# Routing tables of a mixture-of-experts stage: row masks with the pairs innermost, in four pieces

## The chip, the cores and the metric

One core of a Trainium2 chip runs the whole program in one launch. The metric is the time of an execution on the device in microseconds (us); the runs shown are compared by their median. The engines are TensorE (matrix products), Vector, Scalar, GpSimd and Sync (which only issues transfers). In the profile's rows they are PE (PEld for its weight loads), DVE, ACT, POOL and SP.

## The reference

The input has 8 images of 256 channels and 16 x 16 points. A convolution block comes first; its result is added to x. Then every one of the 2048 points is a token of 256 numbers, and a mixture of 8 experts is applied:

```python
S = jax.nn.sigmoid(xt @ Wg)                       # 2048 tokens x 8 experts
G, I = jax.lax.top_k(S, 2)
h = jax.nn.gelu(jnp.einsum('nd,edf->enf', xt, W1) + b1[:, None, :])
y = jnp.einsum('enf,efd->end', h, W2) + b2[:, None, :]
combine = jnp.zeros((N, E)).at[jnp.arange(N)[:, None], I].add(G)
out = jnp.einsum('ne,end->nd', combine, y)
```

So only two experts count for a token. The kernel computes just these: 4096 pairs of a token and a choice.

## The kernel before, in words

**Stages.** The convolution block runs until about 85 us. Then the routing is worked out, and from about 116 us the experts run, tile by tile. Each tile has up to 128 pairs of one expert; there are 39 tiles, and the tables have 40 columns (TCOL). For each tile GpSimd gathers the token rows from memory (`xn_rows`) by row number, TensorE turns them (`turn`), Scalar and Vector round them into a high and a low 16-bit part (`turned_hi`, `rows_T`), TensorE does both layers (`first`, `second`), and GpSimd adds the rows to the output by the same row numbers.

**Routing.** A token sits on a partition (128) in one of 16 blocks (NBLK). With two choices there are 32 pairs per partition, numbered q = choice x 16 + block. Vector works out, for each pair, its tile number and its row in the tile (`place16[:, 1]` and `place16[:, 0]`). Then it builds masks with compares in 16-bit numbers:

- `pay[:, :, 0, :]`: for each pair, 40 numbers, 1 at its tile (L1326). `pay[:, :, 1, :]` is the same times the token's number (L1333), in two halves by choice.
- `hot`: for each pair, 128 numbers, 1 at its row (L1330), in two halves by choice.

TensorE's token table (L839) adds up, over the 32 pairs, hot of a pair (the stationary operand, 128 x 128) times its payload (40 columns). The result has the token's number at each row and tile. Vector turns it into row numbers (`idx`, L1340 and L1342), for which GpSimd's first gather waits (L522). Behind the table TensorE has 16 products of constants that keep it busy (L847), then the first `turn` (L853).

**Later.** The gates of the chosen experts go the same way: Vector multiplies the tile masks by the gates' high and low parts (`gate_pay`, L1369), and a second table with 80 columns (again L839) runs on TensorE ahead of the fourth step of the experts.

**What sets the order.** Each engine has its own list of instructions, in the order of the code, and waits on counters. On Vector, `link` makes an instruction's successor wait for it. Between the row numbers and the first gathered tile Vector splits expert weights into parts (`split_lo`, L972), and Scalar does so ahead of it (`split_hi`, L550). Sync's list (L424 to L446) writes the normalized rows (`rows_out`) and loads the weight quarters of 512 KB (`load`). GpSimd's list begins with memsets, copies the identity (L457) and pads the images (L473).

Of the kernel before, what the change touches and what calls it, by code (L numbers as in the profile page):

```python
# [27 lines left out]
ALU = mybir.AluOpType  # L28
# [3 lines left out]
F16 = mybir.dt.float16  # L32
# [4 lines left out]
P = 128  # L37
# [3 lines left out]
NBLK = NTOK // P  # L41
# [32 lines left out]
NSTG = 4  # L74
# [9 lines left out]
POOL_PADS = 6  # L84

# [21 lines left out]
def build(nc, x_tok, const, const16, params, w1, w2, b2, out):  # L107
    with ExitStack() as ctx:
# [3 lines left out]
        def sem(name):  # L112
            return ctx.enter_context(nc.semaphore(name))
# [47 lines left out]
        def place(n, at, size):  # L161

            return wt[:, n * EXPERT + at:n * EXPERT + at + size]
# [4 lines left out]
        hot = place(3, 0, 2 * NBLK * P).rearrange("p (q r) -> p q r", r=P)  # L168
# [4 lines left out]
        pay = late[:, 0:2560].bitcast(F16).rearrange("p (q v i) -> p q v i", v=4, i=TCOL)  # L173
# [132 lines left out]
        sel_done = sem("sel_done")  # L306
        prefix_mm = sem("prefix_mm")
        pay_done = sem("pay_done")
        hot_done = sem("hot_done")
        table_mm = sem("table_mm")  # L310
# [58 lines left out]
        def _(sp):  # L369
# [80 lines left out]
        def _(pool):  # L450
# [3 lines left out]
            nc.gpsimd.memset(minus_half[:, :], -0.5)  # L454
            g = nc.gpsimd
# [90 lines left out]
        def _(act):  # L546
# [136 lines left out]
        def _(pe):  # L683
# [150 lines left out]
            def table(v, n, bank):  # L834

                for k in range(2 * NBLK):
                    if k % NBLK == 0:
                        pe.wait_ge(hot_done, k // NBLK + 1 if v == 1 else 3)
                    m = pe.matmul(ps[:, bank, 0:n * TCOL], hot[:, k, :], pay[:, k, v:v + n, :].rearrange("p v i -> p (v i)"),  # L839
                                  start=(k == 0), stop=(k == 2 * NBLK - 1))  # L840
                m.then_inc(table_mm, 1)

            table(1, 1, 7)


# [106 lines left out]
            for n in range(TILES + 2):  # L952
                if n == 3:
                    table(2, 2, 7)
                step(n)
# [3 lines left out]
        def _(dve):  # L959
# [347 lines left out]
            def choose(dst, src):  # L1307
# [13 lines left out]
            dve.wait_ge(c16_in, 16)  # L1321
            iota16, tiles16 = c16[:, C16["iota"]], c16[:, C16["tiles"]]
            over_tiles = lambda x, n: x.unsqueeze(2).broadcast_to([P, n, TCOL])
            flat = lambda x: x.rearrange("p a k -> p (a k)")
            link(v.tensor_scalar(place16[:, 0], minus_row, -1.0, None, ALU.mult))
            v.tensor_tensor(out=pay[:, :, 0, :], in0=tiles16.unsqueeze(1).broadcast_to([P, 2 * NBLK, TCOL]),  # L1326
                            in1=over_tiles(flat(place16[:, 1]), 2 * NBLK), op=ALU.is_equal).then_inc(pay_done, 1)
            for a in range(TOP_K):
                half = slice(a * NBLK, (a + 1) * NBLK)
                v.tensor_tensor(out=hot[:, half, :], in0=iota16.unsqueeze(1).broadcast_to([P, NBLK, P]),  # L1330
                                in1=place16[:, 0, a].unsqueeze(2).broadcast_to([P, NBLK, P]), op=ALU.is_equal)
                dve.wait_ge(pay_done, 1)
                v.tensor_tensor(out=pay[:, half, 1, :], in0=pay[:, half, 0, :], in1=over_tiles(tok16[:, :], NBLK),  # L1333
                                op=ALU.mult).then_inc(hot_done, 1)
# [31 lines left out]
            def gate_pay():  # L1366

                for n in (2, 3):
                    ins = v.tensor_tensor(out=pay[:, :, n, :], in0=pay[:, :, 0, :],  # L1369
                                          in1=over_tiles(flat(place16[:, n]), 2 * NBLK), op=ALU.mult)  # L1370
                ins.then_inc(hot_done, 1)
# [133 lines left out]
```

## Time and profile before

| | us |
|---|---|
| median of 3 runs | 338.26 |
| lowest and highest | 337.83, 339.22 |
| the profiled execution | 339.53 |
| its span, first to last instruction | 337.6 |

| engine | busy, share of the span |
|---|---|
| TensorE | 302.4 us, 90% |
| Vector | 249.6 us, 74% |
| Scalar | 179.6 us, 53% |
| GpSimd | 157.1 us, 47% |

The chain that ended last is on TensorE for 73% of the span and on Vector for 13%. TensorE's share is an average: between about 95 and 108 us it does almost nothing, and it is then granted the lower clock of its two. Durations in the rows are those of the profiled execution.

### The profile page before, as it was taken

What the parts mean: (1) busy time and instruction counts of PE and PEld (TensorE: products, weight loads), DVE (VectorE), ACT (ScalarE), POOL (GpSimd) and SP (SyncE); (2) the same over time, 40 slices, a digit from 0 to 9 for tenths busy, and PEclk for the clock granted to TensorE, in tenths of its full rate; (3) what the DMA queues carried; (4) which work ended last, traced back from release to release, by engine and by line L of the source; (5) the groups of instructions that cost most, each with busy time, mean ns of one, the idle gap of its engine ahead of it and who ended that gap; (6) DMA issues with size and microseconds to landing.
All of it is one profiled execution on the core that took longest, in us unless ns stands there. A gap on an engine that the chain in (4) does not pass through costs nothing.

```text
span 337.6 us, 8684 instructions
## 1 busy us (share of the span) xinstructions
PE 302.4 (90%) x3050; PEld 228.4 (68%) x3050; DVE 249.6 (74%) x596; ACT 179.6 (53%) x507; POOL 157.1 (47%) x162
## 2 busy tenths in 40 slices
PE   7999999999412898999999999999999999999960
PEld 7787534567311496888888888888888888877730
DVE  4898796779899699878888888888756464665430
ACT  4557484625816175676666767676444535354310
POOL 2315912456410822664745474757545363544331
PEclk9999999999855799999999999999999999999995
DMA  7500000011578384878687778674353433334310
GB/s 220 173 2 1 2 0 1 0 63 67 190 235 241 80 277 150 206 201 213 188 206 194 214 183 232 160 199 73 76 84 65 81 66 69 70 53 60 55 17 2
DMA packets 36361, 39.41 MB, mean 117 GB/s; under 512 B 8448, under 2 KB 32992, under 8 KB 36320
## 3 DMA queue, kind: packets, MB, share of 16 engines
q1 hardware_dynamic: 29344, 29.56, 29.5%
q0 software_dynamic: 6976, 9.31, 16.1%
q8 instruction: 25, 0.41, 0.5%
q14 instruction: 16, 0.13, 0.1%
HBM read 29.74 MB, written 9.11 MB: 115 GB/s over the span
## 4 chain that ended last, share of the span: by engine, by line
PE 73%; DVE 13%; DMA 8%; issue 2%; ACT 0%; POOLq 0%; SPq 0%; POOL 0%
PE ps L914 16%; PE ps L899 8%; PE ps L903 8%; PE ps L901 8%; PE ps L915 8%; DMA out<-fb,idx 7%; PE ps L758 6%; PE ps L739 4%; PE ps L853 2%; PE ps L767 2%; PE ps L771 2%; PE ps L774 2%; PE ps L847 2%; DMA cst<-const 2%; PE ps L711 1%
## 5 line engine op out<-in xcount | busy, mean ns | idle before, releaser
L676 ACT ACTIVATE fb<-ps,b1t 128x128 f32<-128x128 f32 (+7 forms) x312 | 81.7, 373 | 82.7 <-issue 81.0
L914 PE MATMUL ps<-wt,fb 128*128 x312 | 117.0, 379 | 0.0
L899 PE MATMUL ps<-fb,wt 128*128 128x128 f16 (+7 forms) x624 | 114.3, 214 | 2.6 <-DVE fb L1364 2.6
L903 PE MATMUL ps<-fb,wt 128*128 128x128 f16 (+7 forms) x624 | 114.3, 214 | 0.0
L901 PE MATMUL ps<-fb,wt 128*128 128x128 f16 (+7 forms) x624 | 114.2, 214 | 0.0
L532 POOL DMA_INDIRECT out<-fb,idx x39 | 64.3, 1649 | 93.7 <-DVE s2c L1407 54.8
L915 PE MATMUL ps<-wt,fb 128*128 x312 | 85.0, 272 | 0.0
L899 PEld LDWEIGHTS ps<-fb,wt 128*128 x624 | 61.0, 98 | 32.9 <-issue 3.1
L901 PEld LDWEIGHTS ps<-fb,wt 128*128 x624 | 60.4, 98 | 3.3
L522 POOL DMA_INDIRECT fb<-xn_rows,idx x39 | 50.3, 1291 | 25.3 <-DVE idx L1342 12.8
L903 PEld LDWEIGHTS ps<-fb,wt 128*128 x624 | 60.4, 98 | 0.0
L1394 DVE SCALAR_TENSOR_TENSOR fb<-fb 128x1024 f16<-128x1024 f32 (+7 forms) x39 | 44.2, 1133 | 1.3
L1392 DVE TENSOR_SCALAR fb<-fb 128x1024 f16<-128x1024 f32 (+7 forms) x39 | 25.3, 647 | 26.1 <-ACT fb L676 25.4
L972 DVE SCALAR_TENSOR_TENSOR wt<-wt 128x1024 f16<-128x1024 f32 x32 | 38.1, 1216 | 0.0
L550 ACT ACTIVATE wt<-wt 128x1024 f16<-128x1024 f32 x32 | 34.1, 1100 | 5.9 <-DMA wt<-w 5.9
L1404 DVE SCALAR_TENSOR_TENSOR fb<-b2t,ps 128x256 f32<-128x256 f32 (+7 forms) x39 | 16.3, 419 | 25.9 <-PE ps L915 24.7
L914 PEld LDWEIGHTS ps<-wt,fb 128*128 128x128 f16 x312 | 30.5, 98 | 2.7
L915 PEld LDWEIGHTS ps<-wt,fb 128*128 128x128 f16 x312 | 30.5, 98 | 0.3
L758 PE MATMUL ps<-wt,fb 128*96 128x512 f32 x48 | 21.8, 599 | 0.0
L647 ACT ACTIVATE fb<-ps 128x256 f16<-128x256 f32 (+7 forms) x39 | 16.0, 411 | 10.4 <-PE ps L853 10.4
L500 POOL TENSOR_TENSOR fb<-cst,fm 128x256 f32<-128x256 f32 x16 | 10.7, 689 | 21.9 <-PE ps L774 12.9
L1407 DVE CUSTOM_DVE_ANT_0 fb<-ps,fb,gates 128x256 f32<-128x256 f32 (+7 forms) x39 | 18.8, 483 | 1.4
(208 smaller groups left out, 390.4 us busy)
## 6 DMA issues: line engine op xcount, KB each, us to landing
wt<-w SPq DMA_DIRECT2D x32, 512.0 KB, 4.2
b2t<-b SPq DMA_DIRECT2D x39, 128.0 KB, 3.4
out<-xt SPq DMA_DIRECT2D x8, 256.0 KB, 2.1
xn_rows<-wt SPq DMA_DIRECT2D x8, 256.0 KB, 3.3
xt<-x_tok SPq DMA_DIRECT2D x4, 256.0 KB, 4.7
xt<-x_tok SPq DMA_DIRECT2D x2, 512.0 KB, 7.6
b1t<-params SPq DMA_DIRECT2D x39, 4.0 KB, 2.4
fb<-xn_rows,idx POOLq DMA_INDIRECT x39, 3.7
```

Of the source, the lines that this page charges most:

```text
L522: nc.gpsimd.indirect_dma_start(out=xg[0:ROWS[i], g, :], out_offset=None, in_=xn_rows, in_offset=bass.IndirectOffsetOnAxis(ap=idx[0:ROWS[i] ...
L532: nc.gpsimd.indirect_dma_start(out=out, out_offset=bass.IndirectOffsetOnAxis(ap=idx[0:ROWS[i], i:i + 1].bitcast(U32), axis=0), in_=yb[0:RO ...
L550: nc.scalar.activation(quarter(h, 0), staged(h), ACT.Copy, scale=WS).then_inc(hi_done, 1)
L676: a = nc.scalar.activation(hid[:, s, f * P:f * P + ROWS[n]], h_ps(s)[:, f * P:f * P + ROWS[n]], ACT.Gelu_apprx_tanh, bias=b1t[:, n % NBIAS ...
L758: m = pe.matmul(ps[0:96, TAP_BANK[u], :], tapw[:, k, :], xln_pad[:, 2 * u:2 * u + 2, 1:1 + H, k:k + W], start=(k == 0), stop=(k == TAPS - 1))
L899: pe.matmul(dst, hi, xT[:, s, c * P:c * P + rows], start=(c == 0 and f % 4 == 0), stop=False, skip_group_check=True)
L901: pe.matmul(dst, hi, xT[:, s, (2 + c) * P:(2 + c) * P + rows], start=False, stop=False, skip_group_check=True)
L903: m = pe.matmul(dst, lo, xT[:, s, c * P:c * P + rows], start=False, stop=(c == DC - 1), skip_group_check=True)
L914: pe.matmul(y_ps(s), hhi[:, s, f * P:(f + 1) * P], w, start=(f == 0), stop=False)
L915: m = pe.matmul(y_ps(s)[:, 0:C], hlo[:, s, f * P:(f + 1) * P], hi, start=False, stop=(f == FC - 1))
L972: v.scalar_tensor_tensor(out=quarter(h, 1), in0=staged(h), scalar=WS, in1=quarter(h, 0), op0=ALU.mult, op1=ALU.subtract).then_inc(lo_done, 1)
L1394: v.scalar_tensor_tensor(out=lo, in0=full_h, scalar=HS, in1=hi, op0=ALU.mult, op1=ALU.subtract)\
```

## The change

`hot` and `pay` change their layout: the pair number q is innermost, so that column r of pair k lies 32 numbers (64 bytes) from column r + 1. The compare's other operand, which was a constant row read again for each pair, is now written out once at the program's start by two iotas on GpSimd (`iota_wide`, 128 x 8, and `tiles_wide`, 40 x 32). The row masks are made in four pieces of 8 pairs, each with a signal of its own, for which the token table waits; the tile mask and the token payload are made whole ahead of them. The gates' payload gets a tile of its own, `gpay`, in which the tile numbers stay innermost, and a signal of its own. Two moves go with it: Sync writes the last block of normalized rows behind two weight quarters and not four, and Scalar does the sigmoid of the logits and the following table load behind two weight quarters and not four.

```diff
+QUART = 2 * NBLK // 4
...
-        hot = place(3, 0, 2 * NBLK * P).rearrange("p (q r) -> p q r", r=P)
+        hot = place(3, 0, 2 * NBLK * P).rearrange("p (r q) -> p r q", q=2 * NBLK)
+        iota_wide = place(3, wide, P * QUART).rearrange("p (r k) -> p r k", k=QUART)
+        tiles_wide = place(3, wide + P * QUART, TCOL * 2 * NBLK).rearrange("p (i q) -> p i q", q=2 * NBLK)
...
-        pay = late[:, 0:2560].bitcast(F16).rearrange("p (q v i) -> p q v i", v=4, i=TCOL)
+        pay = late[:, 0:1280].bitcast(F16).rearrange("p (v i q) -> p v i q", v=2, i=TCOL)
+        gpay = late[:, 1280:2560].bitcast(F16).rearrange("p (q v i) -> p q v i", v=2, i=TCOL)
...
-            for h in range(NSTG):
+            for h in range(DC):
                 load(h)
             rows_out(B - 1)
+            for h in range(DC, NSTG):
+                load(h)
...
+            nc.gpsimd.iota(iota_wide, [[1, P], [0, QUART]], base=0, channel_multiplier=0,
+                           allow_small_or_imprecise_dtypes=True)
+            nc.gpsimd.iota(tiles_wide, [[1, TCOL], [0, 2 * NBLK]], base=0, channel_multiplier=0,
+                           allow_small_or_imprecise_dtypes=True).then_inc(wide_set, 1)
...
-            for h in range(QUARTERS_FIRST):
+            for h in range(DC):
                 split_hi(h)
             act.wait_ge(logit_done, 2)
             nc.scalar.activation(sgl[:, :, :], lg[:, :, :], ACT.Sigmoid, scale=1.0 / XS).then_inc(sigl_done, 1)
             nc.scalar.activation(scrap[:, :], eps_c, ACT.Gelu_apprx_tanh)
+            for h in range(DC, QUARTERS_FIRST):
+                split_hi(h)
...
+                    if k % QUART == 0:
+                        pe.wait_ge(hot_done, k // QUART + 1)
+                    m = pe.matmul(ps[:, 7, 0:TCOL], hot[:, :, k], pay[:, 1, :, k], start=(k == 0), stop=(k == 2 * NBLK - 1))
...
+                pe.wait_ge(gpay_done, 1)
+                for k in range(2 * NBLK):
+                    m = pe.matmul(ps[:, 7, 0:2 * TCOL], hot[:, :, k], gpay[:, k, :, :].rearrange("p v i -> p (v i)"),
...
-            for a in range(TOP_K):
-                half = slice(a * NBLK, (a + 1) * NBLK)
-                v.tensor_tensor(out=hot[:, half, :], in0=iota16.unsqueeze(1).broadcast_to([P, NBLK, P]),
-                                in1=place16[:, 0, a].unsqueeze(2).broadcast_to([P, NBLK, P]), op=ALU.is_equal)
...
+            over_tiles = lambda x: x.unsqueeze(1).broadcast_to([P, TCOL, 2 * NBLK])
+            dve.wait_ge(wide_set, 1)
+            v.tensor_tensor(out=pay[:, 0], in0=tiles_wide, in1=over_tiles(flat(place16[:, 1])),
+                            op=ALU.is_equal).then_inc(pay_done, 1)
+            dve.wait_ge(pay_done, 1)
+            v.tensor_tensor(out=pay[:, 1].rearrange("p i (a k) -> p i a k", a=TOP_K),
...
+            for j in range(4):
+                part_of = slice(j * QUART, (j + 1) * QUART)
+                v.tensor_tensor(out=hot[:, :, part_of], in0=iota_wide,
+                                in1=flat(place16[:, 0])[:, part_of].unsqueeze(1).broadcast_to([P, P, QUART]),
+                                op=ALU.is_equal).then_inc(hot_done, 1)
...
-                    ins = v.tensor_tensor(out=pay[:, :, n, :], in0=pay[:, :, 0, :],
-                                          in1=over_tiles(flat(place16[:, n]), 2 * NBLK), op=ALU.mult)
+                    ins = v.tensor_tensor(out=gpay[:, :, n - 2, :], in0=pay[:, 0].rearrange("p i q -> p q i"),
+                                          in1=flat(place16[:, n]).unsqueeze(2).broadcast_to([P, 2 * NBLK, TCOL]),
+                                          op=ALU.mult)
```

On Vector, the list between the places of the pairs and the row numbers was this (`place` holds tile and row numbers, `c` the 16-bit constants, `wt` the space where masks and payloads lie):

```order
L1325 TENSOR_SCALAR place<-gates 128x32 [waits c16_in,dve_step]
L1326 TENSOR_TENSOR wt<-c,place 128x32x40 [waits dve_step]
L1330 TENSOR_TENSOR wt<-c,place 128x2048
L1333 TENSOR_TENSOR wt<-wt,tok 128x16x40 [waits pay_done]
L1330 TENSOR_TENSOR wt<-c,place 128x2048
L1333 TENSOR_TENSOR wt<-wt,tok 128x16x40 [waits pay_done]
L1337 TENSOR_TENSOR lg<-lg,trs 128x128 [waits trs_done]
```

The same place on Vector now (line numbers are those of the changed kernel):

```order
L1345 TENSOR_SCALAR place<-gates 128x32 [waits dve_step]
L1347 TENSOR_TENSOR wt<-wt,place 128x1280 [waits wide_set,dve_step]
L1350 TENSOR_TENSOR wt<-wt,tok 128x1280 [waits pay_done]
L1355 TENSOR_TENSOR wt<-wt,place 128x128x8 x4
L1360 TENSOR_TENSOR lg<-lg,trs 128x128 [waits trs_done]
```

Both payload instructions now stand ahead of the row masks, and the masks are four.

On TensorE, the token table and what follows it stood so:

```order
L839 MATMUL ps<-wt 128x40 [waits hot_done]
L839 MATMUL ps<-wt 128x40 x15
L839 MATMUL ps<-wt 128x40 [waits hot_done]
L839 MATMUL ps<-wt 128x40 x15
L847 MATMUL ps<-c 128x512 x16
```

And on TensorE now:

```order
L854 MATMUL ps<-wt 128x40 [waits hot_done]
L854 MATMUL ps<-wt 128x40 x7
L854 MATMUL ps<-wt 128x40 [waits hot_done]
L854 MATMUL ps<-wt 128x40 x7
L854 MATMUL ps<-wt 128x40 [waits hot_done]
L854 MATMUL ps<-wt 128x40 x7
L854 MATMUL ps<-wt 128x40 [waits hot_done]
L854 MATMUL ps<-wt 128x40 x7
L869 MATMUL ps<-c 128x512 x16
```

The 32 products now have four waits, 8 products behind each.

On GpSimd, the start of the list now has three more rows (before, the instruction ISA stood just ahead of the first multiplication, L485, and the copies of `cst` and `fb` followed on the memsets):

```order
L462 MEMSET wt 128x256
L463 MEMSET minus_half 128x16
L464 ISA
L464 IOTA wt 128x1024
L466 IOTA wt 128x1280
L470 COPY wt<-cst 128x2x128 [waits cst_in]
L486 COPY wt<-fb 128x2x16x16 [waits tr_copied,pad_zero]
```

The ISA and both iotas now stand ahead of the first copy, which waits for a constant.

## Rows read from the trace of the kernel before

**Rows 1.** Chain that ended last, 84 to 135 us (start us, us, what).

```profile
101.06 1.49 DVE wt L1326
102.55 2.20 DVE wt L1330
104.75 0.73 DVE wt L1333
...
108.49 0.71 PE ps L839 x16
109.20 6.00 PE ps L847 x16
```

**Rows 2.** Groups by shape on Vector, 90 to 140 us (busy us, mean ns | idle before).

```profile
L1330 DVE TENSOR_TENSOR wt<-c,place 128x2048 f16<-128x2048 f16 x2 | 4.6, 2286 | 0.0
L1369 DVE TENSOR_TENSOR wt<-wt,place 128x1280 f16<-128x1280 f16 x2 | 2.9, 1484 | 0.0
L1392 DVE TENSOR_SCALAR fb<-fb 128x1024 f16<-128x1024 f32 x4 | 2.8, 688 | 0.1
...
L1326 DVE TENSOR_TENSOR wt<-c,place 128x1280 f16<-128x1280 f16 x1 | 1.5, 1492 | 0.0
```

**Rows 3.** Timeline of Vector, 109 to 116 us (start, us, line, form [idle before <-releaser]).

```profile
109.47 0.26 DVE L1342 SCALAR_TENSOR_TENSOR idx<-ps,cst,found 128x40 int32<-128x40 f32 x1
...
115.87 0.42 DVE L1364 TENSOR_TENSOR fb<-ps,fb 128x256 f16<-128x256 f32 x1 [2.74 <-ACT fb L647]
```

**Rows 4.** Timeline of TensorE, 128 to 131 us: the gate table and the next step.

```profile
128.21 1.31 PE L839 MATMUL ps<-wt 128*128 128x80 f16 x32
130.81 0.22 PE L899 MATMUL ps<-fb,wt 128*128 128x128 f16 x1 [1.29 <-DVE fb L1364]
```

**Rows 5.** Weight loads of 32-bit numbers (timeline), then busy times and clock (PEclk) by stretch.

```profile
5.20 0.53 PEld L697 LDWEIGHTS ps<-par,fb 128*128 128x128 f32 x4
...
5.00:6.00 1.00, 1.00 (x11) 1.00 (x11) 0.46 (x3) 0.47 (x3) 0.00 (x0) 1.00 0.72 217
92.00:114.00 22.00, 7.42 (x61) 4.06 (x62) 19.70 (x50) 7.52 (x10) 4.95 (x6) 0.50 0.71 208
114.00:116.00 2.00, 1.42 (x7) 0.63 (x5) 0.13 (x1) 0.38 (x1) 1.42 (x2) 0.94 0.31 78
```

**Rows 6.** Timeline of GpSimd, at the start and up to the first gather.

```profile
7.90 0.40 POOL L457 COPY wt<-cst 128x256 f32<-128x256 f32 x1 [5.61 <-DMA cst<-const]
9.31 0.62 POOL L473 COPY wt<-fb 128x512 f32<-128x512 f32 x1 [1.01 <-ACT fb L587]
...
12.52 0.95 POOL L476 MEMSET fb<- 128x1024 f32 x1
...
30.15 7.02 POOL L485 TENSOR_TENSOR wt<-wt 128x256 f32<-128x256 f32 x10 [3.48 <-ACT wt L561]
...
110.04 1.95 POOL L522 DMA_INDIRECT fb<-xn_rows,idx  x1 [12.79 <-DVE idx L1342]
```

**Rows 7.** Tile xn_rows, issue to landing: the last write, then the first gathers.

```profile
DMA to landing us min/median/max: 7.8/7.8/7.8
...
DMA to landing us min/median/max: 2.7/3.7/4.1
```

**Rows 8.** Timeline of Scalar, 14 to 16 and 105 to 109 us.

```profile
15.02 0.58 ACT L587 ACTIVATE fb<-ps 128x512 f32<-128x512 f32 x1
...
105.83 1.06 ACT L550 ACTIVATE wt<-wt 128x1024 f16<-128x1024 f32 x1 [1.29 <-DMA wt<-w]
...
108.99 1.28 ACT L661 ACT_TABLE_LOAD   x1
```

**Rows 9.** Reductions over PSUM on Vector: one line's eight, and a timeline row.

```profile
L1215 DVE TENSOR_REDUCE wt<-ps x8: 157/178/192, 68.2 to 89.6; 128x16 f32<-128x32 f32 x8
...
42.88 0.28 DVE L1158 TENSOR_REDUCE s2s<-ps 16x16 f32<-16x128 f32 x1 [2.36 <-PE ps L782]
```

**Rows 10.** Chain that ended last, 11 to 18 us.

```profile
11.65 1.97 DVE wt L1004 x2
```

More of the change, by code:

```diff
@@ L306, in build @@
         sel_done = sem("sel_done")
+        wide_set = sem("wide_set")
         prefix_mm = sem("prefix_mm")
@@ L309, in build @@
         hot_done = sem("hot_done")
+        gpay_done = sem("gpay_done")
         table_mm = sem("table_mm")
@@ L832, in _, with token_table, gate_table @@
             m.then_inc(prefix_mm, 1)
-            def table(v, n, bank):
+            def token_table():
                 for k in range(2 * NBLK):
-                    if k % NBLK == 0:
-                        pe.wait_ge(hot_done, k // NBLK + 1 if v == 1 else 3)
-                    m = pe.matmul(ps[:, bank, 0:n * TCOL], hot[:, k, :], pay[:, k, v:v + n, :].rearrange("p v i -> p (v i)"),
+                    if k % QUART == 0:
+                        pe.wait_ge(hot_done, k // QUART + 1)
+                    m = pe.matmul(ps[:, 7, 0:TCOL], hot[:, :, k], pay[:, 1, :, k], start=(k == 0), stop=(k == 2 * NBLK - 1))
+                m.then_inc(table_mm, 1)
+            def gate_table():
+                pe.wait_ge(gpay_done, 1)
+                for k in range(2 * NBLK):
+                    m = pe.matmul(ps[:, 7, 0:2 * TCOL], hot[:, :, k], gpay[:, k, :, :].rearrange("p v i -> p (v i)"),
                                   start=(k == 0), stop=(k == 2 * NBLK - 1))
                 m.then_inc(table_mm, 1)
-            table(1, 1, 7)
+            token_table()
             for k in range(16):
@@ L953, in _ @@
                 if n == 3:
-                    table(2, 2, 7)
+                    gate_table()
                 step(n)
@@ L1320, in _ @@
                                         op0=ALU.subtract, op1=ALU.subtract))
-            dve.wait_ge(c16_in, 16)
-            iota16, tiles16 = c16[:, C16["iota"]], c16[:, C16["tiles"]]
-            over_tiles = lambda x, n: x.unsqueeze(2).broadcast_to([P, n, TCOL])
+            over_tiles = lambda x: x.unsqueeze(1).broadcast_to([P, TCOL, 2 * NBLK])
             flat = lambda x: x.rearrange("p a k -> p (a k)")
             link(v.tensor_scalar(place16[:, 0], minus_row, -1.0, None, ALU.mult))
-            v.tensor_tensor(out=pay[:, :, 0, :], in0=tiles16.unsqueeze(1).broadcast_to([P, 2 * NBLK, TCOL]),
-                            in1=over_tiles(flat(place16[:, 1]), 2 * NBLK), op=ALU.is_equal).then_inc(pay_done, 1)
-            for a in range(TOP_K):
-                half = slice(a * NBLK, (a + 1) * NBLK)
-                v.tensor_tensor(out=hot[:, half, :], in0=iota16.unsqueeze(1).broadcast_to([P, NBLK, P]),
-                                in1=place16[:, 0, a].unsqueeze(2).broadcast_to([P, NBLK, P]), op=ALU.is_equal)
-                dve.wait_ge(pay_done, 1)
-                v.tensor_tensor(out=pay[:, half, 1, :], in0=pay[:, half, 0, :], in1=over_tiles(tok16[:, :], NBLK),
-                                op=ALU.mult).then_inc(hot_done, 1)
+            dve.wait_ge(wide_set, 1)
[3 more added lines that the diff above has]
+            v.tensor_tensor(out=pay[:, 1].rearrange("p i (a k) -> p i a k", a=TOP_K),
+                            in0=pay[:, 0].rearrange("p i (a k) -> p i a k", a=TOP_K),
+                            in1=tok16[:, :].unsqueeze(1).unsqueeze(1).broadcast_to([P, TCOL, TOP_K, NBLK]), op=ALU.mult)
+            for j in range(4):
[3 more added lines that the diff above has]
+                                op=ALU.is_equal).then_inc(hot_done, 1)
             dve.wait_ge(trs_done, B)
```

3 lines of the change are left out of this document (2 added, 1 removed).

## The prediction

> **What bounds the kernel now.** I read the chain of waits first, because the change sits in one short stretch of it. From 101.06 us the chain runs through Vector alone: L1326, then twice the pair L1330 and L1333, until TensorE starts the second half of the token table at 108.49; then come 0.71 us of table and 6.00 us of filler products (L847) [rows 1]. So each microsecond taken from Vector here reaches the table's end. Second I read the groups by shape for what one instruction costs. All the 16-bit two-input operations run at the same slope: (2286 - 1492) / (2048 - 1280) = 1.034 ns per element plus 169 ns [rows 2]. That is about one element per Vector cycle. In the chain each takes some 0.08 us less than its record, since the next starts that much earlier [rows 1, 2]. Third, the end of this stretch: the row numbers are ready at 109.47 + 0.26 = 109.73, and Vector waits 2.74 us before its first work on a gathered tile [rows 3]. From there its list is full, so a shift of that point shifts what follows.
>
> **The change part by part.** *Vector, the masks.* Before: 1.49 + 2 x (2.20 + 0.73), about 7.4 us from 101.06 to 108.43. Now there are six instructions: the tile mask and the token payload (1280 elements each) and four row masks of 128 x 8 = 1024. In every removed one an input repeats one number innermost; in every new one all three operands lie side by side innermost. No row of this kernel shows such an operation, so it has two bounds. At one element per cycle the lengths are 1.49, 1.41, then 4 steps of 0.169 + 1.06 - 0.08 = 1.15, and the last ends at 101.06 + 1.49 + 1.41 + 4.60 + 0.08 = 108.6, as before. At two per cycle 1280 elements take 0.169 + 0.66 = 0.83 us and 1024 take 0.70 (step 0.62): 101.06 + 0.83 = 101.89, token payload to 102.64, first row mask ready at 103.34, last at 102.64 + 4 x 0.62 + 0.08 = 105.18. I take two per cycle: L1392, with packed operands, moves 1024 elements in 688 ns, which is half the slope of the rows above [rows 2], so the engine has such a rate and the repeat is what all the slow rows share.
>
> The Trainium skill, VectorE: DVE Perf Modes, "The perf-mode tier table", gives a 16-bit tensor_tensor of 2048 elements 1224 ns in place of 2293 if all operands are packed. Its slow figure agrees with the 2286 ns row, and no run here shows its fast one; by it the 6656 elements would save 3.5 us.
>
> *TensorE, the token table.* It still makes 32 products, but in four groups behind four signals, so 8 and not 16 are left after the last mask. Sixteen took 0.71 us and the gate table's 32 took 1.31 [rows 1, 4], so one costs 0.0375 after a fixed 0.11. Now each weight tile hot[:, :, k] is read with 64 bytes from column to column, and so is the payload column. No row shows such a read. Bounds for one product: below 0.0375 (the jump is free); above 0.53 / 4 = 0.13 us, four weight loads of 32-bit numbers at clock 1.00, and twice that, 0.27, at the 0.50 that is granted here [rows 5]. I take 0.06, nearer to the row of the same type and size. TensorE then keeps up with masks every 0.62 us (8 x 0.06 = 0.48), and the table ends at 105.18 + 0.06 + 0.11 + 8 x 0.06 = 105.83 and not 109.20: 3.4 us earlier (3.55 to a loss of 2.8).
>
> *What is late next.* The row numbers come at 106.36, the first gather is issued at 106.67 and lands 3.7 us later (2.7 to 4.1), at 110.4 [rows 3, 6, 7]. The fillers keep TensorE until 105.83 + 6.00 = 111.8, so they, not the gather, still set the first turn, and the whole 3.4 us passes. Up to 114 us the fillers ran at 0.50, the level of 1.2 GHz: TensorE was busy for 7.4 of the 22 us before; then the grant rose to 2.4 GHz [rows 5]. If it rises earlier in the fillers, the gather caps the further gain at 1.4 us; if it stays low through all 16, they take about 7.2 us and 1.2 is lost. I take neither.
>
> *The moved transfer and weight splits.* The gather also waits for the last block of normalized rows. Its write took 7.8 us from issue behind four 512 KB weight loads, landing near 107.9 [rows 7]. Now two of those loads stand behind it; it lands earlier, and even at 107.9 a gather would be in by 111.6, under the fillers. The third quarter's conversion, at 105.83 before, now follows the sigmoid (logits near 105.4) and the table change of 1.28 us, so it ends near 108.3 [rows 8]; Vector wants it after two splits, near 108.7, and has the 2.74 us wait as cover behind it [rows 3]. Cost: nothing; with that cover gone, each 0.1 us is 0.1 us. The dropped wait for the 16-bit constants had long been met; nothing. The bias loads stand behind the same bytes as before; nothing.
>
> *Gates' payload and table.* The two multiplications now read with a 64-byte jump innermost, one input still repeats, 1280 elements each: 1.48 us as before [rows 2], or up to twice the slope, 2 x 1.33 = 2.65 us more in a stretch in which Vector has no wait. I take no change: a reduction over PSUM that jumps 544 bytes at every element (L1215) takes 0.178 us for 32 elements, and one over 128 adjacent elements takes 0.28 (L1158) [rows 9]; that is 1.06 ns per element between them, with nothing left for a jump. Its table at clock 1.00 goes from 1.31 to 0.11 + 32 x 0.06 = 2.0 us, inside the 1.29 us that TensorE then waits for Vector [rows 4]; at 0.13 it would cost 1.7.
>
> *GpSimd at the start.* It gets two iotas, 2304 elements, and an unnamed ISA instruction moves from ahead of L485 to ahead of them. GpSimd is free from 2.29 us; its next work waits for a constant until 7.90 [rows 6]. The iotas cost between a memset's 0.93 ns and a two-input operation's 2.7 ns per element: 2.1 to 6.2 us. The ISA took at most 3.48 us before L485 [rows 6]. So GpSimd is free again between 4.4 and 12.0 us; I take the middle, about 8, ahead of the first copy's 9.31. At 12.0 the copies and the memset end at 14.6, not 13.5, and the normalization beside them on the chain, 1.97 us for a pair [rows 10], would end up to 1.1 later. Scalar's wait for the first copy is at 15.02 [rows 8], still met.
>
> **Sum.** Profiled execution 339.53 - 3.4 = 336.1 us. The median of the runs, 338.26, lies 1.27 lower; I take the shift off it: 334.9.
>
> **The rivals.** *Compares stay at one element per cycle.* For it: every 16-bit two-input row does. Against it: all of them have the repeat. Vector ends at 108.6 and the shorter last group gives 0.1 back: 338.2.
>
> *Jumps of 64 bytes halve Vector's reads.* The place is the gates' payload, 2.65 us at a point from which Vector's delay goes to TensorE whole (it waits for Vector at 130.81 [rows 4]); 3.4 - 2.65 leaves 0.75: 337.5. Rows 9 speak against it, though they read PSUM and 4-byte numbers. The rule for this stands in the Trainium skill, Advanced Engine Details and Errata, "SBUF Cachelines": a read that enters another 16-byte line each time is slower, and two hits per line are wanted. No row here shows SBUF so read by Vector over enough elements to test it.
>
> *Weight loads with a jump become the bound (the slower side).* Place: both tables. The token table ends at 103.40 + 0.11 + 32 s; together with the gate table at half of s it decides against the change from s = 0.17 us. At the upper bound, 0.27 and 0.13, the token table ends at 112.0 (+2.8) and the gate table adds 2.9 less the 1.29 of waiting (+1.6): 342.7. For it: nothing but the missing row; against it: only 32-bit tiles load that slowly here.
>
> *GpSimd's start.* The ISA now falls where the inputs stream in. At four times its old bound (13.9 us) and iotas of 4.1, GpSimd is free at 20.3, its first copy ends at 20.3 + 0.40 + 0.62, Scalar is 6.3 us late, and 3.4 comes off: 341.2. It decides from 17.4 us on. Against it: the old bound.
>
> **How the numbers follow.** Forecast 0.65; one element per cycle 0.11; halved reads 0.13; slow weight loads 0.06; GpSimd 0.05. The forecast's own range is 333.3 (clock back early, free jumps) to 336.3 (part of the losses of clock and start). The range of 8 in 10 goes to 338.6, to take in the two cases near no change with the spread of the runs, and leaves out the two slower ones. This kernel's measurement can tell about 0.5%, 1.7 us: faster means under 336.6, slower over 339.9. Faster 0.63 of the forecast and 0.04 of the middle cases; slower 0.09 and a little of the rest.
>
> **What would show it.** Six Vector instructions of about 0.83 and 0.70 us from 101 us on, the last ending near 105.2, confirm the first step; 1.49 and 1.23 refute it. The products of the token table 0.04 to 0.08 us apart within a group of 8, and the first row numbers near 106.4, confirm the second. Gate payload at 1.4 to 1.5 us each, the fillers ending before 112, the first turn about 3.4 us earlier, the chain at 11 to 18 us unchanged, and GpSimd's first copy still near 9.3 are the rest. The prediction is wrong if the gather becomes the later of the two at the first turn because it waits for the rows' write, or if Vector's list after 112 gets a new wait that gives the shift back before 131.

## The result, and the profile after

The changed kernel takes 339.90 us in the median of 15 runs (338.94 to 342.33), against 338.51 us for the kernel before in the same rounds (15 runs, 337.83 to 339.41). The ratio is 1.0041, interval 1.0026 to 1.0055: slower by 0.4%, where 334.9 us was forecast. The profiled execution took 342.33 us (span 340.5) and is the longest of the 15; so sizes below are taken from rows where two traces hold the same piece of work, and from medians where they are about the end.

The chain that ended last, 100 to 135 us (start us, us, what), answers to [rows 1]:

```profile
101.03 0.84 DVE wt L1347
101.88 0.82 DVE wt L1350
102.71 0.61 DVE wt L1355
103.37 2.94 PE ps L854 x32
...
107.14 5.25 DMA fb<-xn_rows,idx
112.43 0.45 PE ps L875 x2
...
123.47 4.49 DVE wt L1392 x2
127.96 1.13 DVE wt L994
```

Vector is on the chain for the first 2.3 us only; then TensorE's table is, and behind it, in place of the fillers (the products of constants that keep TensorE busy) of [rows 1], the first gather. Further on stands a piece that nobody waited for before: the gates' payload.

The groups by shape on Vector, 90 to 140 us (busy us, mean ns | idle before), answer to [rows 2]:

```profile
L1392 DVE TENSOR_TENSOR wt<-wt,place 128x1280 f16<-128x1280 f16 x2 | 4.6, 2329 | 0.0
L1355 DVE TENSOR_TENSOR wt<-wt,place 128x1024 f16<-128x1024 f16 x4 | 2.5, 684 | 0.0
...
L1347 DVE TENSOR_TENSOR wt<-wt,place 128x1280 f16<-128x1280 f16 x1 | 0.8, 825 | 0.0
L1350 DVE TENSOR_TENSOR wt<-wt,tok 128x1280 f16<-128x1280 f16 x1 | 0.8, 824 | 0.0
```

The masks run at (825 - 684) / 256 = 0.55 ns per element, half of the 1.034 before. The payload of the gates, the same 1280 elements as before, goes from 1484 to 2329 ns each, 1.69 us for the two.

TensorE's timeline (the first three rows around the first turn, the last two around the fourth step, these for [rows 4]):

```profile
103.37 2.93 PE L854 MATMUL ps<-wt 128*128 128x40 f16 x32 [8.11 <-DVE wt L1355]
106.12 4.63 PE L869 MATMUL ps<-c 128*128 128x512 f16 x16
112.43 0.44 PE L875 MATMUL ps<-cst,fb 128*128 128x128 f32 x2 [1.68 <-DMA fb<-xn_rows,idx]
...
128.01 2.19 PE L861 MATMUL ps<-wt 128*128 128x80 f16 x32 [0.56 <-DVE wt L1392]
131.57 0.22 PE L921 MATMUL ps<-fb,wt 128*128 128x128 f16 x1 [1.37 <-DVE fb L1387]
```

The fillers are done at 110.75 and TensorE waits 1.68 us for the gather; ahead of the fourth step it waits twice. After both places the granted clock falls. TensorE by stretch (stretch in us, length, busy, clock, DMA share, GB/s), for [rows 5]:

```profile
108.00:110.00 2.00, 2.00 (x11) 0.95 0.65 75
110.00:112.00 2.00, 0.75 (x4) 1.00 0.68 139
...
114.00:115.00 1.00, 1.00 (x18) 1.00 0.44 131
115.00:116.00 1.00, 1.00 (x13) 0.51 0.07 16
...
118.00:119.00 1.00, 1.00 (x17) 0.78 0.91 356
...
131.00:132.00 1.00, 0.43 (x7) 1.00 0.83 324
132.00:133.00 1.00, 1.00 (x11) 0.54 0.01 4
...
134.00:135.00 1.00, 1.00 (x9) 0.50 0.98 385
135.00:136.00 1.00, 1.00 (x10) 0.75 0.36 94
```

At 115 and at 132 us it is 0.50, the 1.2 GHz level, for some 3 us each time. The kernel before had 1.00 in all of this time:

```profile
116.00:140.00 24.00, 21.99 (x310) 1.00 0.65 197
```

Vector's timeline, for [rows 3]: the row numbers come 2.90 us earlier, the first work on a gathered tile 2.55.

```profile
106.57 0.26 DVE L1365 SCALAR_TENSOR_TENSOR idx<-ps,cst,found 128x40 int32<-128x40 f32 x1
...
113.32 0.42 DVE L1387 TENSOR_TENSOR fb<-ps,fb 128x256 f16<-128x256 f32 x1 [3.09 <-ACT fb L660]
```

GpSimd, for [rows 6]: the iotas end at 5.62 us, the first copy and pad copy begin at 7.86 and 9.27 as before, and the normalization of [rows 10] keeps its 1.97 us.

```profile
2.32 1.94 POOL L464 IOTA wt<- 128x1024 f16 x1
4.24 1.38 POOL L466 IOTA wt<- 128x1280 f16 x1
7.86 0.40 POOL L470 COPY wt<-cst 128x256 f32<-128x256 f32 x1 [2.24 <-DMA cst<-const]
9.27 0.68 POOL L486 COPY wt<-fb 128x512 f32<-128x512 f32 x1 [1.02 <-ACT fb L600]
```

Last, for [rows 7]: tile xn_rows, issue to landing of the first gather alone; it was 3.7 before.

```profile
DMA to landing us min/median/max: 5.2/5.2/5.2
```

### The profile page after: what moved, and what is told of

The parts are those of the page before. It is cut to its first block, busy times and chain, and to the rows that moved or that the text cites. A ratio compares the mean times of both kernels' runs of the same rounds, so it can differ in the third digit from the quotient of the medians.

```text
span 340.5 us, 8687 instructions
## 1 busy us (share of the span) xinstructions
PE 307.3 (90%) x3050; PEld 233.4 (69%) x3050; DVE 248.6 (73%) x597; ACT 179.2 (53%) x507; POOL 155.7 (46%) x164
## 4 chain that ended last, share of the span: by engine, by line
PE 73%; DVE 10%; DMA 10%; issue 2%; ACT 1%; POOLq 0%; SPq 0%; POOL 0%; ACTq 0%
PE ps L936 16%; PE ps L921 9%; PE ps L923 9%; PE ps L925 9%; PE ps L937 8%; DMA out<-fb,idx 7%; PE ps L773 6%; PE ps L754 4%; PE ps L875 2%; PE ps L782 2%; PE ps L786 2%; PE ps L789 2%; DMA cst<-const 2%; DMA fb<-xn_rows,idx 2%; PE ps L726 1%
## 5 line engine op out<-in xcount | busy, mean ns | idle before, releaser
L921 PE MATMUL ps<-fb,wt 128*128 128x128 f16 (+7 forms) x624 | 116.4, 216 | 2.7 <-DVE fb L1387 2.7
L923 PE MATMUL ps<-fb,wt 128*128 128x128 f16 (+7 forms) x624 | 116.3, 216 | 0.0
L925 PE MATMUL ps<-fb,wt 128*128 128x128 f16 (+7 forms) x624 | 116.3, 216 | 0.0
L545 POOL DMA_INDIRECT out<-fb,idx x39 | 61.5, 1577 | 102.7 <-DVE s2c L1431 64.7
L921 PEld LDWEIGHTS ps<-fb,wt 128*128 x624 | 61.8, 99 | 33.1 <-issue 3.4
L923 PEld LDWEIGHTS ps<-fb,wt 128*128 x624 | 61.2, 99 | 3.5
L925 PEld LDWEIGHTS ps<-fb,wt 128*128 x624 | 61.2, 99 | 0.0
L535 POOL DMA_INDIRECT fb<-xn_rows,idx x39 | 48.4, 1242 | 24.0 <-issue 11.3
L1431 DVE CUSTOM_DVE_ANT_0 fb<-ps,fb,gates 128x256 f32<-128x256 f32 (+7 forms) x39 | 18.8, 483 | 1.4
```

The source lines that it names most:

```text
L535: nc.gpsimd.indirect_dma_start(out=xg[0:ROWS[i], g, :], out_offset=None, in_=xn_rows, in_offset=bass.IndirectOffsetOnAxis(ap=idx[0:ROWS[i] ...
L545: nc.gpsimd.indirect_dma_start(out=out, out_offset=bass.IndirectOffsetOnAxis(ap=idx[0:ROWS[i], i:i + 1].bitcast(U32), axis=0), in_=yb[0:RO ...
L921: pe.matmul(dst, hi, xT[:, s, c * P:c * P + rows], start=(c == 0 and f % 4 == 0), stop=False, skip_group_check=True)
L923: pe.matmul(dst, hi, xT[:, s, (2 + c) * P:(2 + c) * P + rows], start=False, stop=False, skip_group_check=True)
L925: m = pe.matmul(dst, lo, xT[:, s, c * P:c * P + rows], start=False, stop=(c == DC - 1), skip_group_check=True)
```

## The experiments

To compare executions whose earlier stages differ by up to 1.2 us, the table gives times from the start of the prefix sums (TensorE, about 94 us) in each profiled execution, and the medians of all runs (the first y is Vector's first work on an expert's output, L1407, now L1431; the end is that of the span). A row's own median and that of the kernel before beside it come from the same rounds; medians of different rows mostly do not:

| kernel | row numbers | first turn | first y | end | median us | the kernel before, same rounds |
|---|---|---|---|---|---|---|
| before | 15.63 | 20.94 | 38.40 | 243.50 | 338.51 | |
| changed | 12.77 | 18.37 | 39.19 | 246.44 | 339.90 | 338.51 |
| e3, fillers ahead of step 4 | 12.73 | 17.94 | 37.15 | 242.64 | 338.82 | 339.10 |
| e5, payload without jumps | 12.73 | 17.83 | 35.43 | 240.21 | 337.02 | 338.84 |
| e7, before with fillers | 15.63 | 19.68 | 37.20 | 242.67 | 338.51 | 338.84 |
| e10, three late biases | 12.74 | 17.29 | 36.45 | 241.51 | 337.58 | 338.82 |
| e13, gather and clock | 12.76 | 16.81 | 36.02 | 241.55 | 337.52 | 338.89 |
| e12, all three | 12.73 | 16.77 | 34.37 | 239.49 | 335.87 | 338.89 |

Two differences between these times, here and in the traces of the other runs, tell more than the medians. From the first turn to the first y it is 17.5 us in the kernel before and 17.6 in e5 and e12, where the payload has no jumps; it is 19.2 in e2, e3, e4, e6, e10 and e13, which keep them; only in the changed kernel, whose clock also fell in the first layer, is it 20.8. From the first y to the end it is 206.4 to 207.3 us in the four profiled executions in which the clock fell at the fourth step (changed, e2, e4, e6) and 204.5 to 205.8 in the twelve others.

All are edits of the changed kernel but e7 and e14. The theories at the start: A, three losses (a lower clock in the first layer, the payload, a lower clock at the fourth step); B, the payload's jumps alone, with the clock an accident; C, weight loads with jumps hold the fourth step.

**e1: jumps moved from Vector to TensorE.**

```diff
-        gpay = late[:, 1280:2560].bitcast(F16).rearrange("p (q v i) -> p q v i", v=2, i=TCOL)
+        gpay = late[:, 1280:2560].bitcast(F16).rearrange("p (v i q) -> p v i q", v=2, i=TCOL)
```

> The changed kernel, but the gates' payload keeps the pairs innermost too (no 64-byte jump on Vector; TensorE reads the payload's 80 columns with the jump). Theory A (the changed kernel loses in three places: the first layer at the lower clock after a wait for the gather, 1.6 us; the gates' payload on Vector, 1.7 us; a second stretch at the lower clock at 132 to 136 us, 1.7 us): payload 0.82 us each and not 2.28, the wait of TensorE ahead of the fourth step shrinks, the clock stays at 1.00 at 128 to 138 us, 3 to 4.5 us less than the changed kernel: 335.5 to 337. Theory B (only the jump on Vector costs, the clock is an accident): 2.9 us less, the stretch at the lower clock stays. Theory C (the tables on TensorE with their 64-byte column jump are what holds the fourth step): 0.5 us less at most, since the gate table gets slower still.

340.65 us, ratio 1.0052 (1.0033 to 1.0072): a miss. Vector's and TensorE's timelines show why:

```profile
121.62 1.55 DVE L1392 TENSOR_TENSOR wt<-wt,place 128x1280 f16<-128x1280 f16 x2
```

```profile
125.52 4.95 PE L861 MATMUL ps<-wt 128*128 128x80 f16 x32
```

The payload falls to 1.55 us for the two, but with both operands jumping a product of the gate table takes 155 ns (4.95 / 32) in place of 41 before (1.31 / 32, [rows 4]); Vector then waits 2.87 us for the table. Every us that Vector won is lost again on TensorE.

**e2: 24 fillers instead of 16 (L869).**

> The changed kernel with 24 filler products and not 16 behind the token table, so that TensorE is busy until the first gather lands. Theory A: the clock stays at 1.00 through the first layer (3.2 us from its start to the first GELU and not 5.4), 1.6 us less than the changed kernel: 338.3; where the fillers run at the lower clock for longer, they end after the gather and take back up to 1.4. Theory B: the same time or up to 1.4 us more.

341.27 us, 1.0065 (1.0044 to 1.0086). The fillers now end at 112.91 and set the first turn at 112.74, where they overlap it; there is no wait and no fall in the first layer. But the clock falls ahead of the fourth step all the same, 0.50 from 130 to 133 us. The time is the one of B (up to 1.4 more) and not A's 338.3. The traces of e1, e3, e4 and e6 have no fall in the first layer either, behind waits for the gather of 0.19 to 1.29 us; so theory A's first loss, 1.6 us, is seen in one execution only, the profiled one of the changed kernel, and how many of its other runs have it is not shown.

**e3: six fillers behind the gate table.**

```diff
                 if n == 3:
                     gate_table()
+                    for k in range(6):
+                        pe.matmul(ps[:, 6, :], c16[:, C16["ones"]], c16[:, 0:512], start=True, stop=True)
```

> The changed kernel with 6 filler products (1.3 us at the full clock) behind the gate table, ahead of the fourth step, into an unused bank. Theory A: TensorE's idle time at 130 to 131.5 us goes, the clock does not fall at 132 to 136 us, 1.5 us less than the changed kernel: 338.4. Theory B: no change, 339.9. If the short idle time is not what lowers the clock, but the slow weight loads of the table or the longer wait at 127 to 128 us, then the clock falls all the same: 339.9 or 0.3 more.

338.82 us, 0.9999 (0.9987 to 1.0010), and the 12 runs lie within 338.51 to 339.54. TensorE's timeline and its clock at the place where it fell:

```profile
128.02 1.47 PE L978 MATMUL ps<-c 128*128 128x512 f16 x6
```

```profile
132.00:133.00 1.00, 1.00 (x14) 1.00 0.89 344
```

That is nearer to A's 338.4 than to B's 339.9, and B falls. The changed kernel's own 15 runs can be parted in seven from 338.94 to 339.54, within e3's range, and eight from 339.90 up. The fall of the clock at the fourth step is a loss of 1.1 us between the two medians, and busy-work there removes it. The two were measured in different rounds; against the kernel before in the same rounds, they lie 1.4 above and 0.3 below.

**e4: SyncE's write of the last rows behind four weight loads again.**

> The changed kernel with the last block of normalized rows written behind four weight loads again, as before the change. Theory A: the gather now sets the first turn (1.68 us wait for it), so it waits for the write near 107.9 and comes about 0.8 us later: 340.7. The prediction's view (the fillers cover it): no change, 339.9.

341.03 us, 1.0071 (1.0043 to 1.0098). The chain of this kernel (start us, us, what):

```profile
108.58 3.86 DMA fb<-xn_rows,idx
```

The gather now starts 1.44 us later, since it waits for that write, and lands at 112.44, the same time as in the changed kernel, because it takes 3.86 us and not 5.25. What holds it is therefore not the time of its issue. The time is near A's 340.7, but A's reason, a later gather, is not in the trace, and the interval overlaps that of the changed kernel (1.0026 to 1.0055). This was the first sign of theory D below.

**e5: the mask a second time, for the gates.**

```diff
+            link(v.tensor_tensor(out=gpay[:, :, 0, :], in0=c16[:, C16["tiles"]].unsqueeze(1).broadcast_to([P, 2 * NBLK, TCOL]),
+                                 in1=flat(place16[:, 1]).unsqueeze(2).broadcast_to([P, 2 * NBLK, TCOL]), op=ALU.is_equal))
             rows_T(0)
...
-                for n in (2, 3):
-                    ins = v.tensor_tensor(out=gpay[:, :, n - 2, :], in0=pay[:, 0].rearrange("p i q -> p q i"),
+                for n in (3, 2):
+                    ins = v.tensor_tensor(out=gpay[:, :, n - 2, :], in0=gpay[:, :, 0, :],
```

> The changed kernel, but Vector writes the tile mask a second time with tile numbers innermost, in its wait for the first turn (110 to 113 us in the trace of the changed kernel, about 3 us idle; such a product took 1.48 us in the kernel before), and the gates' payload reads that copy without jumps. Theory A (Vector is busy without a pause from 119 us to the first y, so each us of the payload reaches the end, and the wait of TensorE before the fourth step, at which the clock fell, goes with it): the payload goes from 4.57 to about 2.9 us, the wait before the fourth step from 1.37 to about 0.3 us, the first y comes some 2.9 us ahead of the kernel before, and the median is 336.0 to 336.8. Rival B (what is gained up to the first y is lost behind it, in the steady steps or the tail): 338 to 339. Rival C (the gate table's strided weight loads, 2.2 us instead of 1.3, set the fourth step): the wait stays, 337.5 or more.

337.02 us, 0.9957 (0.9942 to 0.9972): faster than both, if 0.2 us over the range. On Vector the copy (L1400) is hidden in the wait, the payload is back to its old length, and on TensorE the wait ahead of the fourth step is nearly gone:

```profile
109.23 1.49 DVE L1400 TENSOR_TENSOR wt<-c,place 128x1280 f16<-128x1280 f16 x1
...
120.44 2.89 DVE L1393 TENSOR_TENSOR wt<-wt,place 128x1280 f16<-128x1280 f16 x2
```

```profile
126.94 0.22 PE L921 MATMUL ps<-fb,wt 128*128 128x128 f16 x1 [0.43 <-DVE fb L1388]
```

**e6: the gate table's weights without the jump.**

```diff
-  hot[:, :, k]
+  hot[:, 4 * k:4 * k + 4, :].rearrange("p r q -> p (r q)")
```

> The changed kernel, with the gate table's weights read as 128 consecutive numbers instead of every 32nd (the masks are then mixed, so the gates, and the rows scaled by them, are not those of the reference; the amount of work is the same). Theory C (strided weight loads hold the fourth step): the table goes from 2.2 to about 1.3 us and the median from 339.9 to about 339.0. Theory A (Vector sets the fourth step): the table goes to about 1.3 us, the wait behind it grows by the same 0.9 us, and the median is no better than 339.5; with the longer wait the clock may fall more often, up to 341.

339.88 us, 1.0020 (0.9999 to 1.0042): no sign of the 339.0 that theory C had, and C falls with the trace. The table is back at 1.32 us and the wait behind it is longer by the 0.87 us it saved, so the fourth step begins as long after the table's start as it did (3.55 us, and 3.56 in the changed kernel):

```profile
126.54 1.32 PE L861 MATMUL ps<-wt 128*128 128x80 f16 x32 [0.57 <-DVE wt L1392]
130.09 0.22 PE L921 MATMUL ps<-fb,wt 128*128 128x128 f16 x1 [2.23 <-DVE fb L1387]
```

**e7: e3's six fillers in the kernel before.**

> The kernel before, with the six filler products of 512 columns behind the gate table that made the changed kernel's times narrow. Theory A: the kernel before has no fall of the clock there (1.00 from 128 to 140 us, its wait is one of 1.29 us), so nothing changes: within 0.3 us of the kernel before. If the fillers are worth something of themselves: 338.2 or less. If they hold up the fourth step: 339.5 or more.

338.51 us, 1.0002 (0.9982 to 1.0022): nothing, as A said. Its trace has a use of its own. Its fillers ahead of the first turn took 4.71 us, not 6.17, since the clock rose earlier in them:

```profile
109.36 4.71 PE L847 MATMUL ps<-c 128*128 128x512 f16 x16
```

So the kernel before has a first turn at 19.68 or 20.94 us from the prefix sums, from one execution to the next (20.72 in e14). The same 16 fillers took 4.63 us in the changed kernel, 5.21 in e3, 5.96 in e1 and 6.31 in e9. Which of the fillers and the gather ends last, and so sets the first turn, can thus change from one execution to the next.

**e8: e5, with 26 fillers ahead of the token table and 26 behind it.**

> The kernel of e5 with 26 filler products ahead of the token table (TensorE is idle for 8.1 us there) and 26 instead of 16 behind it, so that the clock is at its upper level at the table and stays there up to the first turn. Theory A (the token table is bound by TensorE's weight loads at the lower clock, 0.088 us a product against 0.064 at the upper one in the gate table): the table ends about 0.5 us earlier, the gather and the first turn too, 335.5 to 336.3. If the fillers outlast the gather, or hold up the table: the first turn later than in e5 by up to 0.6 us, 336.6 to 337.4.

337.74 us, 0.9972 (0.9953 to 0.9991), a miss, over both ranges. The clock is 1.00 at the table, and the table is no shorter:

```profile
103.42 2.86 PE L854 MATMUL ps<-wt 128*128 128x40 f16 x32 [1.50 <-DVE wt L1358]
```

```profile
103.00:106.00 3.00, 2.58 (x31) 1.00 1.08 368
```

So it isn't the clock that sets 0.09 us per product (2.93 / 32 at 0.50, 2.86 / 32 at 1.00). Also, the gather takes 5.3 us here, with the clock at 1.00 all the while.

**Theory D**, after e4 and e8: the gather is late because it shares the queues with the bias loads that SyncE issued from 102 to 106 us. The queues in the time of the first gather, in the kernel before (110.0 to 113.7) and in the changed one (107.1 to 112.4): packets, MB, share of the 16 DMA engines.

```profile
q1 hardware_dynamic: 232, 0.13, 20.8%
q0 software_dynamic: 48, 0.13, 12.2%
```

```profile
q1 hardware_dynamic: 656, 0.33, 53.7%
q0 software_dynamic: 86, 0.26, 14.0%
```

q1 is SyncE's. The last bias is issued at 106.4 and 106.0 us in the two; the gather that comes three us earlier meets three times the packets.

**e9 to e11: biases of tiles 1 to 3 behind the first turn**, in e5's kernel, in the changed kernel alone, and in e5's with 12 fillers.

```diff
-            for i in range(NBIAS):
+            biases(0)
+            sp.wait_ge(xT_mm, 1)
+            for i in range(1, NBIAS):
                 biases(i)
```

> The kernel of e5, in which SyncE issues the biases of tiles 1 to 3 (three loads of 128 KB and three of 4 KB, some 6 us to landing each) only once the first turn is done, instead of between 102 and 106 us. Theory D (the first gather took 3.7 us from its issue in the kernel before, at 110.04 us, and 4.8 to 5.5 us in every kernel with the new masks, because at 107 us it shares the queues with these loads): the first gather takes 3.7 us again, lands at about 111 us instead of 112, and the first turn follows at once or behind the fillers; 0.5 to 1.2 us less than e5: 335.8 to 336.5. Rival E (the gather of the new kernels is late for another reason, so that it lands at 112 whatever else is under way): 4.8 to 5.5 us, and the time of e5, 336.7 to 337.3. If a late bias is waited for by a GELU or a first layer: later than e5.

> The changed kernel with the biases of tiles 1 to 3 issued behind the first turn and nothing else. Theory D: its first gather takes 3.7 us, the first turn comes up to 1.4 us earlier where the fillers are done by then, the wait ahead of the first turn is shorter or gone, and the payload's 1.7 us and the fall of the clock ahead of the fourth step stay: 338.6 to 339.6 against 339.9. Rival E: 339.9.

> The kernel of e9 with 12 instead of 16 fillers. Theory D: if the gather lands at about 111 us, the 16 fillers (4.6 to 6.2 us from 106.1 us) end last in part of the executions, and with 12 (3.5 to 4.9 us) the gather does: up to 0.5 us less than e9, unless the clock falls in the wait. Rival E: no gain over e5, and a longer wait ahead of the first turn, behind which the clock may fall: 337 to 338.5.

The first gather takes 3.7 us again in all three; this is the row of e10:

```profile
fb<-xn_rows,idx POOLq DMA_INDIRECT x1, 3.7
```

e10 is 337.58 us, 0.9970 (0.9955 to 0.9985), a better result than D had room for; e9 is 337.45, 0.9967 (0.9948 to 0.9986), and e11 337.69, 0.9965 (0.9950 to 0.9980), no better than e5: D named the length of the gather rightly and missed all three times. In e9's trace the fillers took 6.31 us and set the first turn, at 18.20 from the prefix sums and so no earlier than in e5 (17.83). Also, the late biases stand ahead of four weight loads in SyncE's list, and Scalar waits:

```profile
123.35 1.06 ACT L565 ACTIVATE wt<-wt 128x1024 f16<-128x1024 f32 x1 [4.10 <-DMA wt<-w]
```

Vector then waits 0.84 us for the second GELU. E, another reason for the late gather, falls; where the biases go instead has a price too.

**e12 to e14: biases of tiles 2 and 3 behind those weight loads**, with e5's payload and 14 fillers; in the changed kernel with e3's fillers; in the kernel before.

```diff
-            for i in range(NBIAS):
+            for i in range(2):
                 biases(i)
             sp.wait_ge(xT_mm, 2)
             for h in range(NSTG, NSTG + QUARTERS_FIRST):
                 load(h)
+            for i in range(2, NBIAS):
+                biases(i)
```

> The kernel of e5 (payload without jumps), with the biases of tiles 2 and 3 issued behind the four weight loads that follow the second turn (in e9 the three late biases stood ahead of these loads, Scalar waited 4.10 us for a weight load and Vector 0.84 us for the GELU behind it), and 14 fillers. If the causes are the three named: the gather takes about 4 us, the first turn comes at 17.0 us from the prefix sums (17.83 in e5), no wait of Vector for the second GELU, the first y at 34.6 (35.43 in e5; 37.20 to 38.40 in the kernel before), and the median is 335.7 to 336.5. If a gain ahead of the first y is taken back behind it: 336.8 to 337.4, as e5 and e9.

> The changed kernel with the biases of tiles 2 and 3 behind the weight loads and the six fillers ahead of the fourth step; the payload keeps its jumps. If the causes add up: e12 plus the payload's 1.6 us less what e12's two fewer fillers bring, 337.0 to 338.0, with a narrow spread as in e3. If the payload's jumps no longer matter once the gather is early (e10 gave 337.58 with them): 336.5 or less.

> The kernel before with the biases of tiles 2 and 3 behind the weight loads, nothing else. Its gather takes 3.7 us already, at a time when the biases are nearly in, and its first turn follows the fillers, so nothing changes: within 0.4 us of the kernel before. If these loads held up the kernel before as well: 338.0 or less.

The edit shown is e12's for the biases; the other two make the same one. All three came out as expected: e12 335.87 us, 0.9911 (0.9887 to 0.9934; 6 runs, 335.50 to 336.15); e13 337.52, 0.9969 (0.9954 to 0.9983); e14 339.02, 0.9995 (0.9976 to 1.0015). The first turn of e12, and the queues from 107.1 to 110.9 us:

```profile
110.88 0.44 PE L877 MATMUL ps<-cst,fb 128*128 128x128 f32 x2 [0.18 <-DMA fb<-xn_rows,idx]
```

```profile
q1 hardware_dynamic: 59, 0.04, 7.9%
```

Step by step: 339.90, with the clock held at the fourth step (e3) 338.82, with the gather freed as well (e13) 337.52, without the payload's jumps (e12) 335.87. That is 1.1, 1.3 and 1.65 us. The table bears out the last two: the first turn 1.13 us earlier from e3 to e13, the first y 1.65 earlier from e13 to e12, at the same first turn. (e12 also has two fillers fewer ahead of the first turn and not the six ahead of the fourth step.) The first two are sizes in this order only: taking the gather first gives 2.3 us (339.90 to e10's 337.58), and then holding the clock 0.1 (to e13's 337.52). Only their sum, 2.4, is the same by both ways.

## Why the prediction was wrong

**Masks: right.** The last mask was to end at 105.18; it ended at 102.63 + 2.49 = 105.12, with both lengths as forecast (0.82 and 0.61). The rule of the Trainium skill (VectorE: DVE Perf Modes, "The perf-mode tier table") agrees: by an estimate at the measured slope its 2048 elements would take 0.825 + 768 x 0.00055 = 1.25 us against its 1.224.

**Token table: the size of s was off.** 0.09 us a product and not 0.06, and the row numbers at 106.83 and not 106.36; the gain is 2.90 and not 3.4. Eight products take 0.73 us, more than the 0.62 between two masks, so TensorE fell behind and set the end. The 0.0375 from which I started mixed two rows that differ in columns (40 and 80) and in clock (0.50 and 1.00). e1 points to the cause that I had not split off: the payload column jumps as well as the weights, and a product with both jumps costs much more than one with the weights' alone (155 against 2.19 / 32 = 68 ns at 80 columns; the token table's 40 columns with both take 89 ns at the same clock, in e8). No run has the token table with one jump alone.

**"The whole 3.4 us passes": failed, at the gather.** I took 3.7 us from issue to landing, as in [rows 7], as if it were the gather's own, and wrote that the bias loads "stand behind the same bytes as before; nothing". Their times did stay; the gather moved 2.9 us towards them. It landed 5.25 us after its issue, at 112.39 and not 110.4, past the fillers on which the step rested, and past the 111.8 that I had for their end. My sign of being wrong named this place for another reason, the write of the rows; but the gather was issued at 107.14, 0.3 us behind the row numbers, so it did not wait for the write. Freed of these loads the gather is worth 1.3 us (e3 to e13), and the kernel before gains nothing by the same edit (e14). In the two profiled executions themselves the first turn came 2.57 us earlier, only 0.3 less than the row numbers; but there the fillers were 1.5 us shorter (4.63 against 6.17), which e7 shows to happen in the kernel before too. That was luck of this execution, and the late gather kept the kernel from having more of it.

**Gates' payload, "I take no change": failed.** It cost 1.69 us in rows, 1.65 at the end (e12 against e13), and 1.6 to 1.7 between the first turn and the first y in six traces (19.2 against 17.5 to 17.6). The rival "jumps halve Vector's reads" had the place and the way right, at two thirds of its price (2.65). My evidence against it, [rows 9], read PSUM in 4-byte numbers and said nothing of 16-bit numbers in SBUF. The rule that I set beside that rival (the Trainium skill, Advanced Engine Details and Errata, "SBUF Cachelines") agrees in direction: two of Vector's reads of 1280 numbers, 64 bytes apart, took 2329 ns each against 1484.

**Gate table: right.** 2.19 us against 2.0 forecast, and no loss from it: e6 takes the 0.87 us away, and its time stays within the changed kernel's spread. The slower rival, slow weight loads, falls with it.

**The clock at the fourth step: not in the forecast.** I had looked at the clock in the fillers only. The payload opened a wait of 0.56 us ahead of the gate table, the wait behind it stayed at 1.37, and the clock fell there in the profiled executions of the changed kernel, e2, e4 and e6. Behind the first y these took 206.4 to 207.3 us, the others at most 205.8. In how many of the changed kernel's runs it fell is not shown; if the two parts of its times are told apart by it, in about half. In the median it is 1.1 us (e3).

**GpSimd: right.** 3.3 us of iotas in the idle time; free at 5.62 and not 8.

Together: 3.4 less 0.5, 1.3, 1.65 and 1.1 makes a loss of 1.15; measured were 1.39. With medians from different rounds (the kernel before had 338.51 to 339.10 in them) each of the terms from medians may be off by some 0.6 us. In the two profiled executions the same account reads: first turn 2.57 us earlier; 3.36 lost from there to the first y, about 1.7 by the payload and 1.6 by the lower clock in the first layer; 2.15 lost behind it, where the clock fell again; the end comes 2.94 us later. e12, with the last three gone, gains 3.0 us over the kernel before, which gains nothing from the fillers (e7) or the later biases (e14); so the masks' gain was there, and the mechanism of that step was right.

**Open.** What decides whether the clock falls at the fourth step. The length of the wait alone doesn't: behind 1.35 us it fell in e4 and not in e10. That e10 gained 2.3 us where e13 shows 1.3 for its gather, and that the six fillers add nothing to it in e13, suggests that the clock fell more seldom in e10; I have no run that shows why.

## What to carry to other kernels

When a piece of the chain gets shorter, ask of the transfer that it releases what else is in the queues at its new time; issue to landing is a property of the moment, not of the transfer. A layout that makes one engine's operands packed makes another reader jump: list every reader of the tile and price each from a row of the same memory and type, and where a cheap second copy fits into a wait, make it. And a wait of TensorE costs more than its length where the clock falls behind it. Last, take more than one profiled execution of the kernel before: its first turn moved by 1.3 us from one to another.

## What the runs showed of the hardware

- A 16-bit product on Vector that reads one operand from SBUF every 64 bytes and repeats the other took 1.57 times as long (2329 against 1484 ns for 1280 elements).
- On TensorE 32 products of 128 x 128 x 80 took 1.31 us with both operands side by side, 2.19 with the weights' columns 64 bytes apart, 4.95 with the moving numbers apart as well; for the token table, with both apart, twice the clock changed nothing (2.93 and 2.86 us).
- A gather of 128 rows of 1 KB needed 3.7 us from issue to landing where SyncE's loads took 7.9% of the DMA engines' time (e12) and where they took 20.8% (the kernel before), and 5.25 where they took 53.7% (the changed kernel).
- The same 16 filler products on TensorE took 4.63 to 6.31 us, depending on when in them the granted clock rose from 0.50 to 1.00.
- Waits of TensorE of 1.33 to 2.23 us ahead of the fourth step were followed by about 3 us at a clock of 0.50 in four profiled executions; in e10 one of 1.35 us was not.
